# A cross network on one core: the last adds of a tile's partial sums moved from GpSimd to one VectorE reduction

## The reference, cut to what matters

```
e = rows of 39 embedding tables, picked by ids           # (1024, 39, 16) float32
xk = x0 = e
for W in (f0, f1, f2):                                   # f1, f2: (128 * 39, 128)
    z  = einsum('bfd,bgd->bfgd', x0, xk)                 # every pair of features
    xk = einsum('bpd,pm->bmd', z.reshape(b, f * g, d), W)
    outs.append(xk)
z = sum over d of concat(outs)                           # (1024, 384)
y = relu(relu([z, dense_ctx] @ W_top1 + b1) @ W_top2 + b2) @ W_top3
```

## Time and profile before

| | |
|---|---|
| three runs | 1392.90, 1393.21, 1393.88 us (median 1393.21) |
| the profiled execution | 1393.13 us |
| its span in the trace | 1391.3 us |
| busy: TensorE / GpSimd / VectorE / ScalarE | 93% / 75% / 70% / 55% |
| granted TensorE clock, mean | 0.998 |

### The profile page before, as it was taken

One profiled execution on the slowest core, in us unless ns is written; L12 is line 12 of the kernel. 1 busy time (PEld: TensorE's weight loads), 2 busy tenths in 40 slices (PEclk: granted clock), 3 DMA queues, 4 the chain that ended last, 5 costly groups with the idle time before them and its releaser, 6 DMA issues.

```text
span 1391.3 us, 25265 instructions
## 1 busy us (share of the span) xinstructions
PE 1294.6 (93%) x5629; PEld 971.1 (70%) x5629; DVE 978.5 (70%) x3241; ACT 760.4 (55%) x2434; POOL 1038.3 (75%) x921
## 2 busy tenths in 40 slices
PE   0179999998999999999999999999999999999999
PEld 0057777776778777877778767877778777877754
DVE  2068778687876878688876778687885878688720
ACT  2136565466655566466664566466664565566631
POOL 7648868788787878788787878878787876566530
PEclk9999999999999999999999999999999999999999
DMA  8131122011211112111211112111211111111000
GB/s 220 25 112 53 47 70 64 6 54 46 80 53 52 47 38 74 27 53 47 79 53 52 47 24 64 50 53 47 78 53 53 46 25 58 51 52 45 1 1 0
DMA packets 73417, 72.97 MB, mean 52 GB/s; under 512 B 32428, under 2 KB 44690, under 8 KB 72716
## 3 DMA queue, kind: packets, MB, share of 16 engines
q1 hardware_dynamic: 60600, 67.88, 16.5%
q0 software_dynamic: 9984, 2.58, 2.2%
q10 hardware_dynamic: 2720, 1.48, 0.4%
HBM read 10.15 MB, written 0.00 MB: 7 GB/s over the span
## 4 chain that ended last, share of the span: by engine, by line
PE 50%; POOL 14%; DVE 11%; issue 10%; DMA 6%; ACT 5%; SPq 3%; DVEq 1%; POOLq 0%; ACTq 0%
PE ps L469 10%; PE ps L473 10%; PE ps L470 10%; PE ps L448 9%; DVE terms L805 9%; POOL terms L364 6%; POOL x_in L341 5%; PE ps L493 5%; DMA x_cols<-x_cols 4%; ACT terms L667 3%; DVE prods L777 3%; PE ps L558 2%; PE ps L483 2%; POOL prods_low L218 2%; DMA x_first<-x_cols 1%
## 5 line engine op out<-in xcount | busy, mean ns | idle before, releaser
L805 DVE SCALAR_TENSOR_TENSOR terms<-ps,x_scal,terms 128x128 f32<-128x128 f32 x2944 | 811.6, 346 | 276.0 <-PE ps L473 149.3
L667 ACT ACTIVATE terms<-ps,x_scal 128x128 f32<-128x128 f32 x2048 | 585.8, 375 | 388.6 <-PE ps L473 342.1
L364 POOL TENSOR_TENSOR terms<-terms 128x1024 f32<-128x1024 f32 (+2 forms) x384 | 565.0, 1471 | 168.2 <-DVE terms L805 142.9
L469 PE MATMUL ps<-w_high,x_high 128*128 128x512 f32 (+1 forms) x1280 | 592.5, 463 | 24.3 <-DVE terms L805 18.6
L473 PE MATMUL ps<-w_high,x_low 128*128 128x512 f32 (+1 forms) x1280 | 499.7, 390 | 6.1 <-ACT x_cols L619 5.6
L470 PE MATMUL ps<-w_low,x_high 128*128 128x512 f32 (+1 forms) x1280 | 497.8, 389 | 0.0
L341 POOL DMA_INDIRECT x_in<-in_tbl,ids_now x312 | 298.9, 958 | 100.5 <-issue 84.6
L469 PEld LDWEIGHTS ps<-w_high,x_high 128*128 128x128 f32 x1280 | 241.4, 189 | 136.5 <-DVE terms L805 50.5
L470 PEld LDWEIGHTS ps<-w_low,x_high 128*128 128x128 f32 x1280 | 242.4, 189 | 71.0 <-issue 29.8
L473 PEld LDWEIGHTS ps<-w_high,x_low 128*128 128x128 f32 x1280 | 241.2, 188 | 60.2 <-ACT x_cols L619 8.2
L448 PE MATMUL ps<-prods,w 117*128 117x512 f32 x262 | 135.3, 601 | 8.6 <-DVE prods L777 8.6
(11 more groups left out here) (45 smaller groups left out, 455.0 us busy)
## 6 DMA issues: line engine op xcount, KB each, us to landing
prods<-x_cols SPq DMA_DIRECT2D x192, 234.0 KB
x_first<-x_cols SPq DMA_DIRECT2D x96, 78.0 KB
x_in<-in_tbl,ids_now POOLq DMA_INDIRECT x312
x_cols<-x_cols SPq DMA_DIRECT2D x14, 312.0 KB
x_diag<-x_scal SPq DMA_DIRECT2D x256, 9.8 KB, 1.9
s<-in_f SPq DMA_DIRECT2D x3, 832.0 KB, 13.2
wt<-in_W_top ACTq DMA_DIRECT2D x1, 768.0 KB, 8.0
wt<-in_W_top ACTq DMA_DIRECT2D x1, 512.0 KB, 9.3
```

Source lines behind the costliest of these rows:

```text
L364: nc.gpsimd.tensor_tensor(t[:, 0:n], t[:, 0:n], t[:, n:2 * n], ALU.add).then_inc(s_tree, 1)
L469: nc.tensor.matmul(y, x1_high[:, par, at:at + P], high, start=True, stop=False)
L667: op = nc.scalar.activation(terms[:, u % 2, FB * ACT_BANKS.index(q) + i, :], ps[:, (BANKS * u + q) % RING, i * G:(i + 1) * G], ACT.Copy, s ...
L805: nc.vector.scalar_tensor_tensor(out=acc, in0=y, scalar=x0, in1=acc, op0=ALU.mult, op1=ALU.add).then_inc(s_mac, 1)
```

## The change

GpSimd's tree ends after two adds, with four partial sums in the slots 0 to 3. VectorE gets a new function `reduce`, which waits for the tree of a tile and for the reader of that x2 buffer, and adds the four slots up to x2 in one tensor_reduce. For its innermost axis the slots are read with a stride of 128 elements (512 bytes). In VectorE's order the reduction of tile u - 1 stands in step u, behind the terms of bank 9 and ahead of the product that is placed after that bank; that of the last tile stands at the end. The semaphore `s_x2` counts the same x2 as before, and those who wait for it are the same.

```diff
-TREE = (8, 4, 2)
+TREE = (8, 4)
+LEFT = TREE[-1]
+REDUCE_AT = 9
...
                     nc.gpsimd.tensor_tensor(t[:, 0:n], t[:, 0:n], t[:, n:2 * n], ALU.add).then_inc(s_tree, 1)
-                pool.wait_ge(s_tree, bt * (STEPS * len(TREE)) + len(TREE) * (u + 1))
-
-                pool.wait_ge(s_s3, bt * STEPS + u - 1 + CREDIT_S3)
-                nc.gpsimd.tensor_tensor(x2[:, u % 2], t[:, 0], t[:, 1], ALU.add).then_inc(s_x2, 1)
...
+            def reduce(bt, u):
+
+                dve.wait_ge(s_tree, bt * (STEPS * len(TREE)) + len(TREE) * (u + 1))
+                dve.wait_ge(s_s3, bt * STEPS + u - 1 + CREDIT_S3)
+                nc.vector.tensor_reduce(x2[:, u % 2], terms[:, u % 2, 0:LEFT, :].rearrange("p t g -> p g t"),
+                                        AX_X, ALU.add).then_inc(s_x2, 1)
...
                     if q in DVE_BANKS:
                         mac(bt, u, q)
+                    if q == REDUCE_AT and u > 0:
+                        reduce(bt, u - 1)
                     if front and (tile, q) in PRODUCTS:
                         multiply(bt, j, PRODUCTS.index((tile, q)), X1_BANK)
...
-            prologue_then_batches(dve, step, prologue, lambda bt: None)
+            prologue_then_batches(dve, step, prologue, lambda bt: reduce(bt, STEPS - 1))
```

## The result

| | before | after |
|---|---|---|
| median | 1393.06 us | 1500.51 us (1499.74 to 1500.80, 4 runs) |
| span of the profiled execution | 1391.3 us | 1498.4 us |
| ratio after / before | | 1.077, 95% interval 1.0752 to 1.0789 |

The change costs 107 us. The forecast said slower, 1472, range 1455 to 1503. The time lies where its second rival (the strided read costs about double, 16%) had put it, 1500.

What follows compares the result with a forecast made beforehand. TensorE, busy 93%, was taken to set the pace. Six batches 65.6, first 7.7, last 8.8, last four tiles 2.5, tail 2.4, less 7.0 give +80.0 us: 1473, stated as 1472, range 1455 to 1503.

Steps and rivals of the forecast that it cites:

- second rival: VectorE's reduction: the strided read costs about double, each boundary grows by 0.44 us more, 28 in all: 1500 us; 16%.
- The wait moved from GpSimd to VectorE, and the gap that it opens: Tile boundaries: ScalarE's bank 0 scaling waits for VectorE's reduction; next terms start 1.91 us after the last, not 0.12 to 0.51.
- the reduction's price: VectorE's new instruction: taken as 0.68 us; price between 0.60 (overlapped with neighbours) and 1.12.
- The sum: A full batch of 16 tiles: delays passed on in first and second tiles of its groups add 10.93 us.
- GpSimd's relief: Two long batches: GpSimd, losing two adds per tile, is no longer late; -7.0 us, a bound from above.
- First and last tiles: Ends of the span: first batch +7.7 us, last batch's three groups with products +8.8, last four tiles +2.5, tail +2.4.
- The fast one: Bank 0 scaling could still start when its bank is ready, VectorE's work hides in idle time: 1386 us; 3%.
- The third: Group starts: only second tiles pay, since idle time elsewhere takes up the first tiles' delays; +40 us: 1433; 8%.
- The fourth: At the reduction: GpSimd late, VectorE waits for the partial sums; only keeps the 7 us: 1479; no separate chance given.

Runs made afterwards that it cites:

- e1_in_order: The changed kernel with the reduction in the same place but reading its 512 inputs in order instead of with a stride; 1468.22 us.
- e6_in_series: Kernel before plus a spare strided reduction on VectorE, for whose end ScalarE's first scaling of a tile waits; x2 still by GpSimd; 1497.58 us.
- e2: Kernel before, no reduction; ScalarE's first scaling of a tile also waits for VectorE's last term of the tile before; 1431.24 us.
- e3: The changed kernel with the reduction moved earlier, behind the terms of bank 6 instead of bank 9; 1411.89 us.
- e4: Kernel before plus a spare strided reduction on VectorE that nobody waits for; x2 still by GpSimd; 1421.20 us.
- e5: Kernel before plus a spare strided reduction nobody waits for; ScalarE's first scaling waits for VectorE's last term of the tile before; 1433.11 us.

## Why the forecast was right in direction and 28 us short

- **The wait moved from GpSimd to VectorE, and the gap that it opens**: right. The gap was put at 1.91 us and is 2.36. Its terms: the reduction's end 0.99 after the last term, not 0.60; ScalarE's start 0.11 later, not 0.05; the scaling 1.14 and the last hand-over 0.12, as taken.
- **The step that failed is the reduction's price**: "I take the lower kind, because ours reads with a stride and writes in order" put it at 0.68 from a row that read in order from PSUM; it is 1.068. ScalarE's strided read the earlier trace rows was no guide to VectorE's from SBUF; the bound of 1.12 from ScalarE's strided write was nearly right. The Trainium skill, SBUF — State Buffer, "Door 1: The DMA port swizzle", has fp32 strides free up to four elements. The runs agree with it: our stride is 128 elements, and against the 0.677 of e1_in_order it costs 0.39 us for 512 elements.
- **The sum**: 10.93 us a batch with the gap of 1.91; 8 boundaries x 0.45 more give 14.5; measured 171.05 - 156.8 = 14.3. That this is so close is in part luck: the eight first and second tiles of tiles 48 to 63 took 15.1 us more, and tile 58, a third tile, 0.9 less (see GpSimd's relief). The other third and fourth tiles kept their own length, as forecast; what they pass on grew by up to 0.2 us.
- **First and last tiles**: tiles 4 to 15 grew by 8.7 us (forecast 7.7), tiles 112 to 123 by 10.7 (8.8). Six boundaries x 0.45 more would give 10.4 and 11.5, so the longer gap covers both; what took the rest off was not followed up. From tile 124 to the end it is 9.6 us, forecast 4.9; the gap explains some 2 of the rest, and the clock the other 3 (below).
- **GpSimd's relief**: the lateness is gone, as the -7.0 had it, but it is not shown that the relief removed it. All six full batches now take 171.0 to 171.1 us; none is late. In e6_in_series, where GpSimd still has its four adds, all six take 171.7 us and ScalarE waits for GpSimd's x2 nowhere: the slower pace alone is enough. And GpSimd was late before in the regular batches too, which the forecast had left out. In tile 58 ScalarE waited for x2, and TensorE then for ScalarE's copy of the transposed rows:

```profile
655.86 0.37 ACT L667 ACTIVATE terms<-ps,x_scal 128x128 f32<-128x128 f32 x1 [3.32 <-POOL x L368]
657.95 0.50 PE L473 MATMUL ps<-w_high,x_low 128*128 128x512 f32 x1 [0.81 <-ACT x_cols L619]
```

The step of that tile was 13.02 us before. It is 12.15 in the changed kernel, 12.20 in e6_in_series, and 11.94 or 11.95 in e2, e3, e4 and e5.
- **Rivals**: the second came true, in its mechanism and in its time. The price was 1.07, not its 1.12; the 63 boundaries x 0.45 make 28 us, the same as its 63 x 0.44, since the hand-overs were longer too. What it had not, the lower clock in the tail (3.4 us) and the shorter tile 58 (0.9 us in a full batch), pulls in opposite directions; that the time still comes out at 1500 is in part luck. The fast one needed ScalarE's scaling to stay beside VectorE's terms; e3_early shows that even where it does, VectorE's instruction still costs more than GpSimd's relief gives. The third (only second tiles pay) is out: first tiles pay 2.2 us. The fourth (VectorE waits for the partial sums) is out: the reduction waited once for GpSimd, 2.9 us.

## What to carry to other kernels

A result that two engines hand to each other should be made as early as its inputs allow, not at the end of the maker's tile: between two waiting engines, work done one after the other cost its whole duration here, while the same work side by side added almost nothing to the wait alone (171.7 against 162.8 us a batch, and 162.7 with the wait alone). Busy shares of 55 to 75% don't show this; the gap from one engine's last instruction of a tile to its first of the next does, and multiplied by the boundaries at which the pacing engine has no slack it gave the time within a few per cent. Before an instruction is moved to VectorE, look at its operands: a strided SBUF read and a second SBUF input beside a GpSimd add each had a price that the neighbouring rows did not show.

## What the runs showed of the hardware that was not expected

- A reduction of 128x512 float32 from SBUF with the inner axis at a stride of 512 bytes took 1.068 us on VectorE, and 0.677 us in order.
- A VectorE add of 128x128 with both inputs in SBUF took 2.32 us on average while GpSimd's 128x1024 add ran, and 0.292 us when it was kept apart. It ended 0.15 us after GpSimd's add. VectorE's terms (one of the two tensors in PSUM) kept their 0.34 us beside it, and the reduction (one input) its 1.07 us beside GpSimd's instructions.
- In the tail of the changed kernel TensorE idled for 2.62 us before it could use x2 of tile 126, and its granted clock then fell. It did so in e1_in_order too, after 2.28 us at the same place (0.57 from 1406 to 1410 us). The stretches around it in the changed kernel (the clock is the third number from the end):

```profile
1432.00:1434.90 2.90, 0.31 (x2) 0.00 (x0) 2.87 (x9) 0.26 (x1) 0.82 (x1) 1.00 0.00 0
1434.90:1438.00 3.10, 3.07 (x5) 1.09 (x6) 0.20 (x1) 0.44 (x1) 2.79 (x2) 0.70 0.00 0
1438.00:1441.00 3.00, 3.00 (x5) 1.19 (x4) 0.82 (x1) 0.00 (x0) 0.00 (x0) 0.50 0.00 0
1441.00:1445.00 4.00, 4.00 (x8) 1.25 (x7) 0.00 (x0) 0.69 (x1) 0.00 (x0) 0.76 0.00 0
1445.00:1460.00 15.00, 15.00 (x35) 6.08 (x34) 0.00 (x0) 3.07 (x5) 0.00 (x0) 1.00 0.00 1
```

0.50 is the 1.2 GHz level. Against the full clock these stretches lose 3.1 x 0.30 + 3.0 x 0.50 + 4.0 x 0.24 = 3.4 us, which is what the time from x2's use to the end has grown by (63.5 against 60.1 us). In e6_in_series, with the gap as long but x2 from GpSimd, TensorE did not stop there and the clock stayed at 1.00; its time from tile 124 to the end is 6 us shorter (93.0 against 99.0), and that more than makes up for its 0.7 us longer batches. What in the idle time lets the clock fall was not tried.
